# A depthwise convolution on TensorE: four full-height taps against four half-width products that carry two taps each

## The reference, cut to what matters

```python
x, z = jnp.split(xz, 2, axis=1)                 # xz = (hidden @ W_in.T) transposed
x = conv_general_dilated(x, conv_w, window_strides=(1,), padding=[(3, 0)],
                         feature_group_count=d_inner) + conv_b[None, :, None]
x = silu(x).transpose(0, 2, 1)
x_dbl = x @ Wx.T                                # gives dt, B and C
h_t = exp(dt_t * A) * h_{t-1} + dt_t * B_t * x_t    # 16 states n per channel
y_t = sum_n(h_t * C_t) + x_t * D
out = (branch(xz) + branch(xz reversed in time, its own weights) reversed back) / 2
```

## Time and profile before

| | |
|---|---|
| median of 3 runs | 3227.04 us (3226.63 to 3227.58) |
| the profiled execution: its own time | 3248.7 us |
| its span, first to last instruction | 3246.9 us |
| busy: PE, DVE, ACT, POOL | 2737.8, 2252.4, 1765.3, 1754.2 us |
| units 0 to 15 (the scans, L884) | 157.4 us to 2180.8 us of the span |
| granted TensorE clock, mean over the span | 0.914 of full |

### The profile page before, as it was taken

How to read it: one execution, slowest core, us unless ns; L and a number is a source line. 1 busy time by engine, 2 the same in 40 slices (tenths; PEclk the granted TensorE clock), 3 DMA queues, 4 the chain that set the end, 5 groups by cost and what they waited for, 6 DMA issues and landing times. The chain is left out here.

```text
span 3246.9 us, 40447 instructions
## 1 busy us (share of the span) xinstructions
PE 2737.8 (84%) x13486; PEld 1826.9 (56%) x13486; DVE 2252.4 (69%) x2812; ACT 1765.3 (54%) x2691; POOL 1754.2 (54%) x554
## 2 busy tenths in 40 slices
PE   5466887887888888878968878777999999999999
PEld 5134665665666565666656656555455555555554
DVE  5287989889889989989988988984442442442430
ACT  1355767758848758758758767641332332322322
POOL 0598868878878878778778887861000000000000
PEclk9777898899999989989989989887999999999999
DMA  6222324333333334333333332323000000000000
GB/s 254 85 69 94 119 101 140 108 109 119 123 106 121 107 104 147 109 105 117 129 115 115 111 134 90 130 89 131 26 33 0 32 32 0 32 18 15 6 7 7
DMA packets 149278, 283.24 MB, mean 87 GB/s; under 512 B 23659, under 2 KB 97878, under 8 KB 149078
## 3 DMA queue, kind: packets, MB, share of 16 engines
q1 hardware_dynamic: 142934, 264.08, 23.8%
q0 software_dynamic: 6144, 16.79, 1.5%
HBM read 239.13 MB, written 41.68 MB: 86 GB/s over the span
## 5 line engine op out<-in xcount | busy, mean ns | idle before, releaser
L708 POOL TENSOR_TENSOR hs<-u,bb 128x2048 f32<-128x2048 f32 x256 | 1159.3, 4534 | 368.5 <-PE hT L1013 323.3
L884 DVE TENSOR_TENSOR_SCAN hs<-dA,hs 128x1024 f32<-128x1024 f32 x512 | 1166.3, 2284 | 122.7 <-POOL hs L708 75.9
L797 ACT ACTIVATE dA<-dt,cols 128x511 f32<-128x511 f32 x1024 | 661.8, 680 | 412.9 <-DVE hs L884 408.6
L1013 PE MATMUL hT<-ident,hs 128*128 128x128 f32 x3584 | 558.4, 297 | 264.2 <-DVE held L894 222.4
L1013 PEld LDWEIGHTS hT<-ident,hs 128*128 128x128 f32 x3584 | 434.9, 151 | 405.6 <-DVE held L894 290.2
L894 DVE SCALAR_TENSOR_TENSOR held<-hT,ct,held 128x512 f32<-128x512 f32 x864 | 603.8, 742 | 54.2 <-PE hT L1013 53.1
L1287 ACT ACTIVATE gl<-bank,cols_sb 128x512 f32<-128x512 f32 x192 | 130.7, 687 | 528.4 <-PE bank L1526 528.1
L1526 PE MATMUL bank<-mT,cms_sb 128*128 128x512 f32 x768 | 363.6, 598 | 10.1 <-ACT mT L1281 8.6
L1032 PE MATMUL moe<-xgT,held 128*128 128x128 f32 x2400 | 334.4, 299 | 30.0 <-ACT xgT L811 28.2
L1032 PEld LDWEIGHTS moe<-xgT,held 128*128 128x128 f32 x2400 | 321.3, 214 | 61.4 <-ACT xgT L811 37.6
L136 POOL COPY cur<-slot 128x8 uint32 (+1 forms) x8 | 1.5, 187 | 640.9 <-DVE held L148 631.3
(11 more groups left out here) (219 smaller groups left out, 3332.1 us busy)
## 6 DMA issues: line engine op xcount, KB each, us to landing
held<-wl SPq DMA_DIRECT2D x75, 1024.0 KB
bb<-b_scratch SPq DMA_DIRECT2D x128, 512.0 KB, 5.6
held<-wl SPq DMA_DIRECT2D x75, 512.0 KB
xg_scratch<-zero SPq DMA_DIRECT2D x10, 960.0 KB, 5.4
xg<-xg_scratch SPq DMA_DIRECT2D x75, 128.0 KB
yg_scratch<-yg SPq DMA_DIRECT2D x75, 128.0 KB, 1.7
held<-x SPq DMA_DIRECT2D x16, 512.0 KB, 8.7
cb<-b_scratch SPq DMA_DIRECT2D x32, 256.0 KB, 4.7
```

What stands on the lines that cost most here:

```text
L708: nc.gpsimd.tensor_tensor(hs[n % HS][:, :, :], u[d][:, :, :], row, ALU.mult).then_inc(dBu_ready, 1)
L797: last = nc.scalar.activation(dst, src, ACT.Exp, scale=cols[:, at:at + 1])
L884: nc.vector.tensor_tensor_scan(h, decay, h, 0.0, ALU.mult, ALU.add).then_inc(scan_done, 1)
L1013: last = nc.tensor.transpose(hT[c % 2][:, k * P:(k + 1) * P], hs[n % HS][:, k, c * P:(c + 1) * P], ident[:, :])
```

## The change

The weights of two neighbouring taps go into one matmul. Its 128 contraction rows are 64 channels twice: on their own 64 partitions as they are, on the other 64 partitions shifted by one step. So there are now two buffers: `xpad[0]` holds channels 0 to 63 of a block on partitions 0 to 63 and the same channels one step later on partitions 64 to 127, `xpad[1]` the same for channels 64 to 127 the other way round. A block's convolution is 2 pairs of taps times 2 halves g of the channels: still 4 matmuls of 512 columns, each with a 128x64 stationary operand, that write PSUM partitions 0 to 63 (g = 0) or 64 to 127 (g = 1) of the bank `prep`.

For that, ACT copies a projected block in two instructions, one per half of the partitions, and SP then copies each half to the other half of the partitions by DMA, two transfers of 128 KB per block (`shift`). PE waits for these (`shifted[k]`) before the d = 0 convolution. In SP's queue the `shift` of blocks 0 and 1 stands at the start of state 0 of an odd unit, that of blocks 2 and 3 at the start of state 3, before the C row of state 4; each waits for `p_used` of its projection. DVE builds 64 tap matrices of 64x64 instead of 32 of 128x128, from a copy `w_tap` of the weights on both halves (4 more small loads at setup), and clears both `xpad` whole instead of their borders.

```diff
-            xpad = s0("xpad", [P, DB, L + 2 * (KC - 1)])
+            xpad = [s0(f"xpad{g}", [P, DB, L + 2 * (KC - 1)]) for g in range(2)]
-            taps = s0("taps", [P, 2 * DB * KC, P])
+            taps = s0("taps", [P, 2, DB, 2, KC // 2, HP])
+            def pair_at(d, q):
+                return 2 * q if d == 0 else 2 * (KC - 1) - 1 - 2 * q
+            def tap_of(d, q, early):
+                return pair_at(d, q) + early if d == 0 else 2 * (KC - 1) - pair_at(d, q) - early
...
+                def shift(k, unit):                       # SP
+                    sp.wait_ge(p_used, use_of("proj", k, 0, unit) + 1)
+                    for g in range(2):
+                        own, other = slice(HP * g, HP * (g + 1)), slice(HP * (1 - g), HP * (2 - g))
+                        sp.dma_start(xpad[g][other, k, KC - 2:KC - 2 + L], xpad[g][own, k, KC - 1:KC - 1 + L]).then_inc(shifted[k], 16)
...
+                for k in range(DB):                       # SP, head, before store_b(0, 0)
+                    shift(k, 0)
...
                         for n in range(NS):
+                            if d == 1 and more:
+                                for what, k in PREP[0][2 * n] + PREP[0][2 * n + 1]:
+                                    if what == "proj":
+                                        shift(k, unit + 1)
...
-                        nc.scalar.activation(xpad[:, k, KC - 1:KC - 1 + L], src[:, :], ACT.Copy).then_inc(p_used, 1)
+                        for g in range(2):                # ACT
+                            own = slice(HP * g, HP * (g + 1))
+                            last = nc.scalar.activation(xpad[g][own, k, KC - 1:KC - 1 + L], src[own, :], ACT.Copy)
+                        last.then_inc(p_used, 1)
...
-                nc.vector.memset(xpad[:, :, 0:KC - 1], 0.0).then_inc(hT_used, 1)
-                nc.vector.memset(xpad[:, :, KC - 1 + L:], 0.0).then_inc(hT_used, 1)
+                for g in range(2):
+                    nc.vector.memset(xpad[g][:, :, :], 0.0).then_inc(hT_used, 1)
                 dve.wait_ge(w_sem, 16 * N_W)
-                for i in range(2 * DB * KC):
-                    nc.vector.tensor_scalar(taps[:, i, :], ident[:, :], cols[:, CW + i:CW + i + 1], None, ALU.mult).then_inc(taps_ready, 1)
+                # for d, k, g, q, half: 64 in all
+                                    nc.vector.tensor_scalar(taps[rows_, d, k, g, q, :], ident[rows_, rows_], w_tap[rows_, g, at:at + 1],
+                                                            None, ALU.mult).then_inc(taps_ready, 1)
...
-                            pe.wait_ge(taps_ready, 2 * DB * KC)
-                        for t in range(KC):
-                            at = t if d == 0 else 2 * (KC - 1) - t
-                            last = mm(dst[:, :], taps[:, (d * DB + k) * KC + t, :], xpad[:, k, at:at + L], start=(t == 0), stop=(t == KC - 1))
+                            pe.wait_ge(taps_ready, 4 * DB * KC)
+                        if d == 0:
+                            pe.wait_ge(shifted[k], 32 * (b + 1))
+                        for q in range(KC // 2):
+                            at = pair_at(d, q)
+                            for g in range(2):
+                                last = mm(dst[HP * g:HP * (g + 1), :], taps[:, d, k, g, q, :], xpad[g][:, k, at:at + L],
+                                          start=(q == 0), stop=(q == KC // 2 - 1))
```

More of the change, by code:

```diff
@@ L19 @@
 HF = DB // 2
+HP = P // 2
 EPS = 1e-5
@@ L205, in bass_mamba_moe_then_linear_attention_mlp @@
         cols = s0("cols", [P, NCOL0])
+        w_tap = s0("w_tap", [P, 2, CB])
         xa = held[:, :].rearrange("p (c d) -> p c d", d=DM)
@@ L210, in bass_mamba_moe_then_linear_attention_mlp @@
         w_sem = sem("weights_in")
-        N_W = 6
+        N_W = 10
         placed, zeroed, grouped = sem("placed"), sem("zeroed"), [sem("grouped_early"), sem("grouped_late")]
@@ L270, in _ @@
                 sp.dma_start(cols[:, :], cols0).then_inc(w_sem, 16)
+                for g in range(2):
+                    for half in range(2):
+                        sp.dma_start(w_tap[HP * half:HP * (half + 1), g, :], cols0[HP * g:HP * (g + 1), CW:CB]).then_inc(w_sem, 16)
                 for d in range(2):
@@ L466, in bass_mamba_moe_then_linear_attention_mlp @@
             setup_v, setup_g, setup_a, taps_ready = sem("setup_v"), sem("setup_g"), sem("setup_a"), sem("taps_ready")
-            xnT_in, p_ps, p_used = sem("xnT_in"), sem("prep_ps"), sem("prep_used")
+            xnT_in, p_ps, p_used, shifted = sem("xnT_in"), sem("prep_ps"), sem("prep_used"), [sem(f"xpad_shifted{k}") for k in range(DB)]
             xc_ready = sem("xc_ready")
@@ L864, in _ @@
                     nc.vector.memset(dA[j][:, :, :], 0.0).then_inc(scan_done, 1)
-                nc.vector.memset(xpad[:, :, 0:KC - 1], 0.0).then_inc(hT_used, 1)
-                nc.vector.memset(xpad[:, :, KC - 1 + L:], 0.0).then_inc(hT_used, 1)
+                for g in range(2):
+                    nc.vector.memset(xpad[g][:, :, :], 0.0).then_inc(hT_used, 1)
                 dve.wait_ge(w_sem, 16 * N_W)
-                for i in range(2 * DB * KC):
-                    nc.vector.tensor_scalar(taps[:, i, :], ident[:, :], cols[:, CW + i:CW + i + 1], None, ALU.mult).then_inc(taps_ready, 1)
+                for d in range(2):
+                    for k in range(DB):
+                        for g in range(2):
+                            for q in range(KC // 2):
+                                for half in range(2):
+                                    rows_ = slice(HP * half, HP * (half + 1))
+                                    at = (d * DB + k) * KC + tap_of(d, q, int(half != g))
+                                    nc.vector.tensor_scalar(taps[rows_, d, k, g, q, :], ident[rows_, rows_], w_tap[rows_, g, at:at + 1],
+                                                            None, ALU.mult).then_inc(taps_ready, 1)
                 dve.wait_ge(setup_a, 1)
```

## The result

The changed kernel is slower: 3272.12 us median (3267.64 to 3276.23, 4 runs) against 3227.31 (3226.63 to 3227.66, 4 runs) for the kernel before, a ratio of 1.014 with a 95% interval of 1.0124 to 1.0156. The forecast of "slower" was right. Its size was not: +45 us instead of +14, outside the range's 3258.

A forecast was written before the change was run, and what follows sets the result against it. DVE was taken to bound the kernel, with PE full but only just in time. Terms of -1 (PE's relief), +12 (block 2's late copy) and +3 (head) gave +14 us on the median: 3241 us, range 3219 to 3258.

The forecast's parts named there:

- DVE sets the pace, PE's relief is worth nothing: Loop: PE relieved of 103 us, worth 0 in odd units and 0.1 us in each of 8 even units, -1 us.
- The halves overlap: Loop convolution on PE: two column halves run at once, 1.72 us instead of 3.44 a block.
- ACT's second copy, blocks 0, 1 and 3, the B and C rows, the setup: Loop and setup: extra ACT instructions, other copies, delayed row loads and small weight loads, each off the path, 0.
- The place and the mechanism of the new wait: Slot 8, seven odd units: PE idles 3 to 3.5 us for block 2's copy, clock drops, DVE waits in slot 9.
- A: Loop: block 2's copy lands late and the clock drops behind it; +8 to +22 us, 3241 us, chance 0.42.
- B: Loop: the wait for block 2's copy is short or the clock stays up; +2 to +8 us, 3232 us, chance 0.26.
- the shift of block 2 lands at about 1349: Unit 9, slot 8: copy lands in issue order behind the tile's weights, at 1348.5 to 1349.5.
- the term of 1.7 us a unit: DVE's loss per odd unit from block 2's late copy, lower clock in most units; 7 x 1.7 = +12 us.
- the bound that I wrote down, 4.3 us a unit: Upper bound of DVE's loss per odd unit, without overlap of halves and at lower clock; 7 x 4.3 = +30 us.
- The head, +3 us: Before the first scan: later start and copies, less relief from shorter convolutions, +3 us; bounds 0 and +8.
- 0.14 x 64 = 8.8 us: Head: DVE builds 64 half-width tap matrices at 0.14 us each; bounds 0.07 and 0.206 each, 4.5 to 13.2 us.
- The base: Starting time: median 3227.04 us, though the profiled execution took 3248.7, with an unexplained 8.49 us head wait carried over.

The follow-up runs named there:

- run 2: Kernel before, with taps 1 and 2 left out of each convolution in the loop, halving PE's instructions there: 3227.09 us, ratio 1.0003.
- run 12: Changed kernel with the head edits of run 10, projections in slots 0, 1, 5, 7 and convolutions in 2, 4, 8, 10: 3225.51 us, ratio 1.0003.
- run 3: Changed kernel without the shift transfers and PE's waits for them, in loop and head: 3239.15 us, ratio 1.0047.
- run 5: Changed kernel, with SP issuing the expert tile's loads after the copies of blocks 2 and 3: 3267.1 us, ratio 1.0054, on a slower chip.
- run 9: Changed kernel without block 3's second copy and its wait in the loop: block 2's second copy landed after 7.06 us on average, against 7.46; no time given.
- run 6: Changed kernel with the 64 tap matrices built grouped by start partition instead of alternating halves: 3283.59 us in one run, on a slower chip.
- run 1: Kernel before, unchanged, profiled once more: ratio 0.9999, span 3226.7 us.
- run 7: Changed kernel with ACT issuing the copies in its own DMA queue instead of SP: 3298.15 us in one run, on a slower chip.
- run 8: Changed kernel with projections in slots 0, 1, 4, 5 and convolutions in 2, 6, 8, 10: 3265.32 us, ratio 1.0058, on a slower chip.
- run 10: Changed kernel, head edits only: grouped tap matrices, first convolution waiting for only 32 of them, only borders of `xpad` cleared: 3260.46 us, ratio 1.0103.

## Why the prediction was right or wrong

**DVE sets the pace, PE's relief is worth nothing: right.** Forecast -1 us of a possible -103; run 2 took 102.5 us off PE for a change of +1 us (-2 to +4), run 12 the same within a version of the changed kernel. The 2 us by which unit 1 is shorter in runs 2, 3, 5 and 12 are the most that the profiles show for the relief.

**The halves overlap: right, with 1.57 us of relief a block and not quite 1.72.** A block takes 1.94 us by itself, 1.98 on average in run 3. Counted as the prediction counted the 3.44, from its start to that of the next instruction, it takes 1.87 us at full clock, 0.15 more than half. The prediction had seen some 0.1 us for a switch of the tiling and left it out of the sum. The same 0.1 stands in the rows here: L1056 starts 0.07 us before the modelled end of L1029 (1369.56 + 3.40 against 1372.89), where it was 0.16 us before it in the earlier trace rows. The ends are modelled, so this price is not shown by itself.

**ACT's second copy, blocks 0, 1 and 3, the B and C rows, the setup: right at 0.** Runs 3, 5 and 12 have them (run 3 without the copies) and are back at the units of before. PE waits for no copy of block 3 in the changed kernel, but these copies delay those of block 2 a little (below).

**The place and the mechanism of the new wait: right.** Block 2's copies behind the tile's loads, PE idle in slot 8, the clock at its lower level behind it, DVE's wait in slot 9, seven times; runs 3 and 5 remove it and the loop's loss with it. In unit 9 the clock was 0.57 over the 3.44 us behind the idle 5.66. The convolution took 3.40 us there and 3.34 to 3.68 in all seven, at or above the top of what I had allowed (3.4). By the rule on idle gaps in the Trainium skill ("TensorE: Matmul & The Clock Gate", HAM oscillation), A was likelier than B; the trace agrees, with 0.50 to 0.57 behind all seven waits.

**The size of that wait: wrong.** The step that failed is "the shift of block 2 lands at about 1349", with its bounds 1348.5 and 1349.5, and with it the term of 1.7 us a unit. Counted from the issue of the B rows ahead of it, that is 5.9 us; the changed kernel needed 9.0 in unit 9 (1360.41 to 1369.42) and 8.5 on average over the seven odd units. PE idled 5.1 us instead of 3 to 3.5, and DVE waited 4.8 us instead of losing 1.7. The odd units grew by less than these 4.8 us, by 3.7 on average: DVE's other waits for transposes in an odd unit fell from 3.95 to 2.7 us. 7 x 3.7 = 26 us where I had 12. The 2.6 us between 5.9 and 8.5 are made up of:

- 0.4 us because I put the landing at 1349.0, when the C row that it was read from had landed at 1349.4.
- 0.4 us from the choice of row. I took unit 9, where the C row landed after 5.81 us. The seven odd units of that same profile run from 5.81 to 7.02, mean 6.25: the one unit I read was the lowest of them. The second profile of the same kernel has a mean of 6.54, and 6.92 in unit 9, so the execution matters as well.
- 0.5 us because a block's copy is two transfers, and the second was issued at 1361.42, not at 1360.90.
- about 0.4 us from block 3's copies (run 9).
- the rest, some 0.8 us, from the copies being slower than a C row of the same 256 KB in a stretch that is already full. Both have packets of 2 KB. In the traces' packets of these stretches one of a copy takes 135 ns (median), one of a C row 84 ns in the kernel before. For the 128 packets of a block on 16 engines that is an estimated 0.4 us more. No run varied this, so this part is argued from the traces and not shown.

I had treated the landing as a matter of order ("in the order of issue"), though the bound that I wrote down, 4.3 us a unit, covers the 3.7 that came. It was a bound for a convolution without overlap of the halves, so that it fits is luck.

**The head, +3 us: wrong.** The term that failed is "0.14 x 64 = 8.8 us", with its bounds of 0.07 and 0.206 each. It took 20.30 us, 0.317 each, above my upper bound: I took 0.206 us for the cost of an instruction, when it was the cost of an instruction that overlaps its neighbours, and the new order takes that overlap away (run 6: 0.163 us with the overlap). The clearing was right (3.6 us against 3.7, and 0.7 of gaps). The copies add 4 us before the last two blocks (in run 3, without them, 14.0 of the 18.3 us stay), where I had given them 3; the overlap gives back as much. Sum: +18 instead of +3.

**The base: without weight in the end.** I carried the "remote" wait over and added the difference to the median, which was right to do; the worry that it might absorb the head's delay was idle, since ordinary executions don't have it (run 1).

Together: -1 + 12 + 3 became 0 + 24.5 + 18.3 - 2.3 (rest of the span) = +40.5 us by the spans, +44.8 by the medians; the 4 us between are the spread of the runs: the profiled execution of the changed kernel is 3.2 us under its median, that of the kernel before 1.2 over.

## What to carry to other kernels

A duration read from a row of back-to-back instructions is a throughput, and holds only for the same pattern; if the change alters the start partitions or the order, the bound has to be the time of one instruction alone. A transfer's landing is to be read from every repetition, and with it the DMA share of the stretch: at a share near 1 another queue didn't help here (run 7), and moving the issue ahead of the burst did (runs 5, 8 and 12). And when an engine is relieved that doesn't set the pace, even a version without new losses may bring nothing, as here (run 12), while each new dependence it needs can cost.

## What the hardware showed unexpectedly

- 64x64 `TENSOR_SCALAR` on DVE: 0.163 us each when they start on the same partition, 0.317 when starts at 0 and 64 alternate. ACT's two copies of 64 partitions each, also alternating, take 0.59 us each, like one of 128 partitions (0.57 in the earlier trace rows).
- A copy of 128 KB from one half of SBUF's partitions to the other lands after 2.2 to 2.4 us when the tile's loads are behind it (block 2 in run 5, DMA share 0.52 in unit 9), and the second copy of block 2 after 6.7 to 8.0 us behind 2 MB of loads (the tile's 1.5 MB and the B rows; up to 8.3 in run 10); issued on ACT's queue the copies take up to 8.6.
- The kernel's head has waits of ACT put down to "remote" in some executions (8.49 and 12.95 us in the first profile; 14.87 and 2.82 in run 5) and none in others. The chip of runs 5 to 8 had them in every profile, and the kernel before was 22 us slower there. What they wait for stays open.
